# Cross-attention and FFN kernel: the mixing weights of 59 of 64 pairs brought to their matrix's diagonal by DMAs of the sync queue

## The reference

```python
x = x + xattn(layernorm(x), ctx, ctx, wq, wk, wv, wo)
x = x + ffn(layernorm(x), W_in, b_in, W_out, b_out)

def xattn(queries, keys, values, wq, wk, wv, wo):      # 16 heads of 16
    Q, K, V = ...                                      # (batch, head, 16, length)
    corr = irfft(rfft(Q, axis=-1) * conj(rfft(K, axis=-1)), n=L, axis=-1)
    top_vals, top_idx = top_k(corr, 4)                 # along the length
    w = softmax(top_vals, axis=-1)
    out = 0
    for i in range(4):
        gather_idx = (arange(16) - top_idx[..., i]) % 16
        out = out + w[..., i, None] * take_along_axis(V, gather_idx[..., None], axis=2)
    return merge_heads(out) @ wo
```

## Time and profile before

| | |
|---|---|
| time, median of 3 runs | 1065.5 us (1065.46 to 1065.85) |
| profiled execution, span from the first to the last instruction | 1064.2 us |
| PE busy | 1047.4 us, 98% |
| DVE busy | 965.1 us, 91% |
| ACT busy | 939.9 us, 88% |
| POOL busy | 505.0 us, 47% |
| ACT copies L756 in all | 256, 78.6 us busy, 307 ns each |
| stage of the pairs, 34 to 550 us | PE 516.00 of 516.00 us busy |

### The profile page before, as it was taken

The page is one execution under the profiler, slowest core; times in us unless marked ns, Lnnn a source line. Parts: engine busy times, 40 slices in busy tenths (PEclk is TensorE's granted clock), DMA queues, the critical chain, the costliest instruction groups (busy, mean ns, idle before and its releaser), DMA issues.

```text
span 1064.2 us, 28999 instructions
## 1 busy us (share of the span) xinstructions
PE 1047.4 (98%) x9358; PEld 778.0 (73%) x9358; DVE 965.1 (91%) x2768; ACT 939.9 (88%) x1697; POOL 505.0 (47%) x674
## 2 busy tenths in 40 slices
PE   8999999999999999999998899999999999999998
PEld 6788888888888888888887444444444888888887
DVE  4789999999988888888889999999997999999998
ACT  5888888899999998888888688888888999999996
POOL 5788888888888888888887400000001000000000
PEclk9999999999999999999999999999999999999999
DMA  5454444334445443444431498999999999999995
GB/s 178 130 150 145 121 121 120 121 120 120 121 120 140 121 120 120 121 120 120 120 111 41 132 325 301 300 305 316 309 300 342 356 347 363 355 354 355 346 364 195
DMA packets 141665, 222.59 MB, mean 209 GB/s; under 512 B 72432, under 2 KB 92272, under 8 KB 137456
## 3 DMA queue, kind: packets, MB, share of 16 engines
q1 hardware_dynamic: 140464, 220.12, 62.8%
q10 hardware_dynamic: 1088, 1.05, 0.3%
HBM read 121.00 MB, written 83.89 MB: 193 GB/s over the span
## 4 chain that ended last, share of the span: by engine, by line
PE 94%; ACT 2%; DVE 2%; issue 1%; DMA 1%; POOL 0%; ACTq 0%; DVEq 0%; POOLq 0%
PE sums L666 21%; PE bank L635 10%; PE sums L635 10%; PE sums L464 8%; PE sums L477 8%; PE bank L515 8%; PE sums L539 7%; PE sums L489 6%; PE bank L527 5%; PE bank L501 5%; PE bank L556 5%; PE sums L672 1%; DMA store_x<-in_L_xattn_wv 1%; ACT arena L756 0%; ACT arena L686 0%
## 5 line engine op out<-in xcount | busy, mean ns | idle before, releaser
L666 PE MATMUL sums<-wout,arena 128*128 128x256 f16 x2048 | 229.8, 273 | 1.2 <-DVE arena L1521 1.2
L666 PEld LDWEIGHTS sums<-wout,arena 128*128 128x128 f16 x2048 | 196.9, 98 | 32.5 <-DVE arena L1514 7.3
L1521 DVE SCALAR_TENSOR_TENSOR arena<-arena,wout_rel 128x512 f16<-128x512 int16 x256 | 180.3, 746 | 2.0 <-ACT arena L935 0.9
L756 ACT ACTIVATE arena<-arena 32x128 f32<-32x128 f32 x256 | 78.6, 307 | 47.8 <-DVE arena L1222 45.5
L635 PE MATMUL sums<-arena,win 128*128 128x512 f16 x512 | 115.9, 379 | 1.0 <-DVE arena L1466 0.9
L635 PE MATMUL bank<-arena,win 128*128 128x512 f16 x512 | 115.7, 379 | 0.0
L686 ACT ACTIVATE arena<-arena 128x512 f16<-128x512 f32 x192 | 112.9, 617 | 1.6 <-POOL arena L998 1.1
L1485 DVE TENSOR_REDUCE hmax_all<-arena 128x1 f32<-128x1024 f32 x96 | 111.3, 1211 | 2.9 <-ACT arena L892 2.9
L935 ACT ACTIVATE arena<-arena,wout_rel 128x512 f16<-128x512 int16 x159 | 106.2, 706 | 0.0
L892 ACT ACTIVATE arena<-sums,b_in_sb,z_scale 128x512 f32<-128x512 f32 x128 | 97.4, 778 | 9.8 <-PE sums L635 4.9
L1088 POOL CAST store_x<-one 128x1 bf16<-128x1 f32 x1 | 0.2, 189 | 220.0 <-DVE one L1503 220.0
(11 more groups left out here) (141 smaller groups left out, 2303.7 us busy)
## 6 DMA issues: line engine op xcount, KB each, us to landing
hidden_scratch<-arena SPq DMA_DIRECT2D x32, 1536.0 KB, 5.5
arena<-hidden_scratch SPq DMA_DIRECT2D x64, 768.0 KB, 6.7
arena<-in_ctx_turned SPq DMA_DIRECT2D x64, 256.0 KB, 2.6
arena<-in_x_turned SPq DMA_DIRECT2D x64, 256.0 KB, 2.9
arena<-in_x SPq DMA_DIRECT2D x64, 256.0 KB, 3.7
x_scratch<-arena SPq DMA_DIRECT2D x64, 256.0 KB, 3.4
arena<-x_scratch SPq DMA_DIRECT2D x32, 512.0 KB, 6.0
out<-arena SPq DMA_DIRECT2D x31, 512.0 KB, 4.2
```

The costliest lines, as they stand in the source:

```text
L666: last = nc.tensor.matmul(bank[m * 2 + k // 2][:, k % 2 * D:(k % 2 + 1) * D], gbuf[:, s, f, k * P:(k + 1) * P], wout16[:, f, :], start=f = ...
L1521: V.scalar_tensor_tensor(gbuf[:, 1, f, :], hq[:, f, :], wout_rel[:, f:f + 1], gbuf[:, 0, f, :], ALU.mult, ALU.subtract).then_inc(S["c_lo"], 1)
```

## The change

For pairs 0 to 58 `spread_blocks` moves from ACT to SP: the four copies become four DMAs of the same shape, [32 partitions x 4 x 32] fp32 from `blocks` to `mt` (128 pieces of 128 bytes each, 16 KB), which count up a semaphore `s_mt` by 16 each. SP issues them in step t for pair t-5, behind `load_x(t)` and ahead of `load_turned(t)`, after it has waited for `bt_done` and `ot_done`. The last five pairs keep the copies on ACT. `attend` and `turn_weights` wait for `s_mt` or, for the last pairs, for ACT's `mt_out`.

```diff
+BY_HAND = 5
...
+        s_mt = sem("s_mt")
...
+        def wait_spread(eng, p):
+
+            if isinstance(p, int) and p < 0:
+                return
+            if p < PAIRS - BY_HAND:
+                eng.wait_ge(s_mt, 64 * (p + 1))
+            else:
+                eng.wait_ge(S["mt_out"], p - (PAIRS - BY_HAND) + 1)
...
+            def spread_blocks(p):
+                if p == 0:
+                    sp.wait_ge(S["mt_zero"], 1)
+                sp.wait_ge(S["bt_done"], p + 1)
+                wait(sp, S["ot_done"], p)
+                for i in range(4):
+                    part = slice(32 * i, 32 * i + 32)
+                    sp.dma_start(mt.rearrange("p c b l -> p (c b) l")[part, :, part], blocks[part]).then_inc(s_mt, 16)
...
                 if active(t, 0) and t >= X_FIRST:
                     load_x(t)
+                if active(t, 5):
+                    spread_blocks(t - 5)
                 if active(t, 0) and t > 0:
                     load_turned(t)
...
             load_x(PAIRS - 1)
+            spread_blocks(PAIRS - 6)
             load_turned(PAIRS - 1)
...
             def attend(p, taken=None):
 
-                pe.wait_ge(S["mt_out"], p + 1)
+                wait_spread(pe, p)
...
             def step(t):
-                if active(t, 4):
-                    spread_blocks(t - 4)
                 if active(t, 1):
                     take_k(t - 1)
...
                 dve.wait_ge(S["w2_done"], p + 1)
-                wait(dve, S["mt_out"], p)
+                wait_spread(dve, p - 1)
```

More of the change, by code:

```diff
@@ L749, in spread_blocks @@
             def spread_blocks(p):
-                if p == 0:
-                    act.wait_ge(S["mt_zero"], 1)
                 act.wait_ge(S["bt_done"], p + 1)
```

## The result

The change makes the kernel slower: 1118.9 us (median of 4 runs, 1114.2 to 1120.7) against 1065.7, a ratio of 1.0492 with a 95% interval of 1.0478 to 1.0506, or about +53 us. The forecast had the sign, the place and the kind of loop, and 1118.9 lies within its range, near the upper end (1120). The size, +25 us, was under half of what came, and nearly every pair is late, where the forecast had half of them; it had itself named lateness in every pair as a sign of being wrong.

What follows compares the result with a forecast made beforehand. TensorE was taken to bound the pairs. Held issues 20.7, the weight-transpose pair 2.5 and FFN weight loads 2.8, less 0.5 at the start, gave 25.5, say +25 us on the median 1065.5: 1090.5 us, range 1067 to 1120.

Steps and rivals of the forecast that it cites:

- lateness in every pair: At attend: a sign that would prove the forecast wrong, against lateness only in pairs with a held issue.
- The bound: Stage of the 64 pairs: TensorE alone sets the pace, 8.89 us per pair, without waiting for ScalarE.
- the worth of what is removed: ScalarE's copies, 1.26 us a pair, 74 us in all: costed at 0, with 0.5 us off at two ends.
- The loop: From attend through ScalarE, GpSimd and SP's transfers to the next attend: a constant lateness is paid anew in each pair.
- One issue takes 0.43 us with 0.05 us between two: SP's queue: price per spread issue, bounds 0.33 and 0.58 us, putting the last of four at 307.83 us.
- no stall there: Attend in an undisturbed pair: weights come at about 310.15 us, 0.2 us before PE wants them.
- It just fits: Undisturbed pair: issue plus landing and the queue behind load_x each give 310.1 us, against attend at 310.38.
- The landing: From the last spread issue until its transfer has landed: 2.3 us taken, with bounds 1.1 and 3.0.
- (a): Rival at attend: the transfers fit and no pair is late; only 0.5 us at the start moves, 1065 us; chance 0.10.
- (b): Rival at attend: the stall is paid once, later pairs are in time; about +2.5, 1068 us; chance 0.06.
- (c): Rival on SP's queue: pieces in flight hold each of the four issues, 2.7 us late per pair; 1225 us; chance 0.08.
- (d): Rival at the stage's end: ScalarE's freed time turns up on PE, 2 to 3 us at most; 1063 us; chance 0.03.

Runs made afterwards that it cites:

- the run without weights: Changed kernel with the spread DMAs removed: pairs 0 to 58 get no weights by copies or DMAs, attend reads zeros; 1065.2 us, ratio 0.9993.
- the run with rows: Changed kernel, but each of the four DMAs writes 32 rows of 512 contiguous bytes instead of 128 pieces of 128 bytes; 1112.5 us, ratio 1.0435.
- the run with thirty pairs: Changed kernel with 30 pairs by DMA instead of 59; the last 34 pairs instead of 5 keep ScalarE's copies; 1093.8 us, ratio 1.0258.
- the run with two issues: Changed kernel, but two of the four blocks of a pair go by DMA and two by ScalarE's copies; 1086.7 us, ratio 1.0189.
- run ahead: Changed kernel, but SP issues the four transfers ahead of store_x1 and load_x of the same step instead of behind them; 1083.1 us, ratio 1.0165.

## Why the prediction missed the size

**The bound, and the worth of what is removed: right.** PE sets the pace, and ScalarE's 1.26 us a pair was hidden; the 0.5 us taken off for the start is there too (in the run without weights the first attend starts at 34.11 against 34.69, and the span is 1063.6 against 1064.2).

**The loop: right, but it is one of two.** It is in the chain of waits link by link, and thirty pairs lose about half of what 59 lose. The loop through PE's inverse and VectorE's transpose was missed; it is level with the other to 0.1 us, so for a pair in which nothing is held it changes the sum by about that.

**The step that failed is "One issue takes 0.43 us with 0.05 us between two".** It was taken from load_x and store_x1, on the condition that the spread's pieces cost SP what theirs do; measured are 0.60 and 0.04 (and by the run with rows the pieces are not why). With it fell "no stall there", the verdict on the undisturbed pair. The three issues ahead of the last one then cost 1.92 us instead of 1.41, 0.5 us in every pair. The upper bound, the row of b_in (0.58), was near the true value, but the sum went by the other.

How much that is can be worked out against load_x_turned, on which SP's order hangs. Forecast: the last issue 307.83 - 305.11 = 2.72 us behind it, attend 310.38 - 305.11 = 5.27 behind it, 0.05 to start, so 2.50 us for the landing and any hold. Measured: 3.33 us to the last issue where nothing is held, 5.42 to an attend that does not wait (208.06 to 213.48), 0.04 to start, so 2.05. The other two terms came out right in the mean. Over the 59 pairs the hold, taken as the time from load_x_turned to the last issue less 3.33, is 0.5 us in the mean; 0.92 in half the pairs was forecast. The time from the last issue until all four have landed is 2.33 in the mean; 2.3 was forecast. That agreement is luck: it is 2.04 in the 27 pairs whose last issue comes over 0.2 us late, 2.57 in the other 32, and no run shows a fixed 2.3. Hold and landing less room: 0.5 + 2.33 - 2.05 = 0.78 us, in nearly every pair (53 of 58 periods are over 0.2 us too long), where 0.2 us to spare in half the pairs was forecast. Take 0.45 us, the missing room, off each of the 58 measured excesses and not below zero, and 30 us of 52.5 are left. This is worked out from the trace, not run, and it is a low figure: the same reckoning gave 8.5 us for the run with two issues, whose periods are 21.1 us too long, since an earlier issue brought little there: the landing took 2.9 us in the median instead of 2.5. The forecast put 26 for that. By this estimate the price of an issue is the larger part of the miss; that it is all of it is not shown.

The last 0.13 us of the 0.91 per pair were not in the sum at all: as far as the rows show, attend takes 1.16 us instead of 1.06 when it has waited, and once the clock fell, as told below.

**"It just fits" was a bad place to stop.** Two limits were each put at 310.1 against 310.38, and their agreement was taken for safety. They are two conditions that must both hold, and with 0.2 us to spare a term mis-sized by 0.17 us, times three, turned half the pairs into nearly all. The experiments take them apart: with one issue, or with two, what is left is the queue (+19 and +21 us); with the queue out of the way what is left is the issues and their holds (+17); with both relieved, +4. The shares overlap, so they do not add up to 53.

**The landing.** The runs show no single figure for it. In the run ahead, where nothing large is ahead, it is 1.8 us at the least and 1.9 in the median; behind store_x1 and load_x the median is 2.5 in the changed kernel, 2.9 for two issues and 3.4 for the one DMA of 128 rows.

**The rivals.** (a) is refuted by the result, (b) by the run with thirty pairs; (c) happens, but in single issues only (the worst 2.43 us), and not by the number of pieces: with a quarter of them, in the run with rows, as many issues are held (19 over 0.3 us longer than usual between 100 and 540 us, in either run); (d) has nothing to come from, as the run without weights shows.

## What to carry to other kernels

Work moved off an engine that is not the bound was worth nothing here by itself (0.7 us), and the new path has to be priced to its last link: the four issues on SP's queue went out one after the other, 0.60 us each and 0.04 between, so the price of one is to be multiplied by how many stand ahead of the last (three, 1.92 us). A transfer on which the bounding engine waits does not belong behind large ones on which it does not: that place cost 36 of the 53 us here. Where a chain closes within one period, any lateness is paid in every period (0.91 us in each of 58 here), and there can be more than one such chain, as the second loop showed; a slack of 0.2 us, against holds of 0.3 to 1.8 us in the changed kernel, is none.

## What the runs showed of the hardware

An issue's time differed with the kind of transfer and with what stood directly ahead of it. Four in a row of 32 partitions within the core's memory take 0.59 to 0.60 us each, whether in 32 or in 128 pieces; one of 128 rows there takes 0.47. The same store_x1 takes 0.33 to 0.34 us where SP had issued nothing for 0.4 us or more before it (seven in the kernel before), 0.43 directly behind load_x_turned and 0.59 directly behind the spread (run ahead, median of 56). Which of partitions and patterns makes the step from 0.47 to 0.60 was not tried.

Some issues are held. Between 100 and 540 us 25 in the kernel before take 0.3 to 2.3 us longer than the median of their line, 18 at store_x1 and 7 at load_x; in the changed kernel it is 19, by 0.3 to 1.8 us, 6 of them at the spread. No load_turned or load_x_turned is among them; there they take 0.59 us at the most in any of the eleven kernels. The traces show what is under way then. One held load_x of the kernel before, in SP's timeline, and two lines of the DMA queues from 119 to 121 us (packets, MB, share):

```profile
119.19 1.43 SPq L310 DMA_DIRECT2D arena<-in_x  x1
```

```profile
q1 hardware_dynamic: 200, 0.38, 76.9%
q8 instruction: 1, 0.02, 3.5%
```

The packet of 16 KB on the queue that the profile calls "instruction" is under way from 119.14 to 120.25 us. In all 25 held issues of the kernel before a packet of an instruction queue is under way during the issue, and 21 of them end 0.32 to 0.39 us after it. Of the other 176 issues 29 have one. In the traces of all eleven kernels it is 216 of 216, against 555 of 3301. The late landings go with it too: all 10 of more than 2.8 us from the last issue in the changed kernel, and all 12 of more than 2.3 us in the run with blocks transposed sooner, have a packet of the 16 KB queue under way in that time, against 2 of the other 49 and none of the other 47. No run moved these packets, so that they cause the holds is not shown by a test.

The clock of TensorE fell for a short while at a long wait of PE. PE's timeline around the pair with the DMA transpose, and the windows view of 6.7 us there:

```profile
370.46 2.08 PE L550 MATMUL bank<-arena,store_x 128*128 128x128 f32 x8 [2.57 <-DMA arena<-arena]
...
382.45 1.06 PE L550 MATMUL bank<-arena,store_x 128*128 128x128 f32 x8
```

```profile
370.10:376.80 6.70, 6.34 (x38) 4.22 (x40) 0.31 (x3) 2.20 (x5) 2.80 (x5) 0.50 0.28 56
```

After 2.57 us without a matmul the granted clock is 0.50 of full speed for these 6.7 us; attend takes 2.08 us instead of 1.06, and the period is 11.99 us without a further wait: 3.1 us beside the stall itself. Not every such wait does this: the attend behind the 2.61 us at 36.31 takes 1.16 us. The kernel before has no such drop in the stage of the pairs.
